# A software pipeline on one core: ScalarE's second exponent ahead of the normalizations, the feed-forward one step later, and GpSimd splitting the negated maxima

## The reference, cut to what matters

```python
x = x + tanh(g_xattn[0]) * L0_xattn(layernorm(x), ctx, ctx)     # 16 heads of 16, softmax, no projections
x = x + tanh(g_ffn[0])   * L0_ffn(layernorm(x), ...)            # scale, round to fp8, 256x256 matmul, rescale, bias
x = x + tanh(g_xattn[1]) * L1_xattn(layernorm(x), ctx, ctx, mask, Wq, bq, Wk, bk, Wv, bv, Wo, bo)
x = x + tanh(g_ffn[1])   * L1_ffn(layernorm(x), weight, gamma, beta)   # fake quantization, ternary weight
```

## Time and profile before

| | |
|---|---|
| median of 3 runs (lowest to highest) | 2249.64 us (2249.06 to 2306.87) |
| profiled execution | 2246.3 us, span 2244.5 us |
| busy: PE, PEld | 1947.8 us (87%), 1429.4 us (64%) |
| busy: DVE, ACT, POOL | 1941.7 us (87%), 1637.9 us (73%), 1122.4 us (50%) |
| first pass, steady part | about 60 to 860 us |
| second pass, steady part | about 890 to 2110 us |

### The profile page before, as it was taken

The page is one execution under the profiler, slowest core; times in us unless marked ns, Lnnn a source line. Parts: engine busy times, 40 slices in busy tenths (PEclk is TensorE's granted clock), DMA queues, the critical chain, the costliest instruction groups (busy, mean ns, idle before and its releaser), DMA issues. The chain is left out here.

```text
span 2244.5 us, 73785 instructions
## 1 busy us (share of the span) xinstructions
PE 1947.8 (87%) x24736; PEld 1429.4 (64%) x24736; DVE 1941.7 (87%) x3958; ACT 1637.9 (73%) x2631; POOL 1122.4 (50%) x1905
## 2 busy tenths in 40 slices
PE   3888888888888886799999999999999999999857
PEld 2665665665665654577777777777777777777545
DVE  4788888888888886589999999999999999999579
ACT  1777777777777776377777777777777777777579
POOL 2566666666666664234444444444444444444310
PEclk8999999999999998799999999999999999999879
DMA  2221211211211110100000000000000000000035
GB/s 79 65 63 59 62 60 59 63 60 59 63 60 59 61 53 13 30 23 24 21 21 21 21 21 21 21 21 21 21 21 21 22 23 21 21 21 18 1 111 189
DMA packets 113869, 95.23 MB, mean 42 GB/s; under 512 B 13440, under 2 KB 113792, under 8 KB 113792
## 3 DMA queue, kind: packets, MB, share of 16 engines
q1 hardware_dynamic: 113792, 94.23, 13.4%
HBM read 60.63 MB, written 33.55 MB: 42 GB/s over the span
## 5 line engine op out<-in xcount | busy, mean ns | idle before, releaser
L844 DVE TENSOR_REDUCE a_nmax<-bank_max 128x8 f32<-128x1024 f32 x512 | 624.8, 1220 | 132.9 <-DVEq L843 127.1
L1113 PE MATMUL bank_max<-UM,U 32*128 32x256 f32 x4096 | 585.7, 403 | 13.7 <-PEq L1226 7.1
L1120 PE MATMUL bank_exp<-UM,U 32*128 32x256 f32 x4096 | 556.7, 389 | 3.9 <-PEq L1261 3.9
L1135 PE MATMUL bank_o<-probs,V 128*17 128x128 f32 x8192 | 325.9, 276 | 170.4 <-PEq L1131 166.3
L641 ACT ACTIVATE probs<-bank_exp 128x1024 f32<-128x1024 f32 x256 | 262.2, 1024 | 272.3 <-ACTq L640 272.3
L1113 PEld LDWEIGHTS bank_max<-UM,U 32*128 32x128 f32 x4096 | 353.1, 185 | 105.6 <-issue 99.6
L1135 PEld LDWEIGHTS bank_o<-probs,V 128*17 128x17 f32 x8192 | 192.0, 96 | 326.2 <-issue 325.4
L530 POOL TENSOR_SCALAR UM<-U,heads_eo 128x512 f32<-128x512 f32 x128 | 88.6, 692 | 605.7 <-POOLq L528 605.7
L1120 PEld LDWEIGHTS bank_exp<-UM,U 32*128 32x128 f32 x4096 | 372.6, 185 | 5.8 <-issue 5.2
L941 DVE CAST bank_max<-ff_qT 128x1024 f32<-128x1024 bf16 x256 | 314.4, 1228 | 8.9
L573 ACT ACTIVATE probs<-bank_exp 128x1024 f32<-128x1024 f32 x256 | 261.8, 1023 | 81.2 <-ACTq L572 81.2
(11 more groups left out here) (168 smaller groups left out, 4252.0 us busy)
## 6 DMA issues: line engine op xcount, KB each, us to landing
X<-in_x SPq DMA_DIRECT2D x128, 128.0 KB, 2.1
ctx<-in_ctx SPq DMA_DIRECT2D x128, 128.0 KB, 2.0
out_y<-U SPq DMA_DIRECT2D x128, 128.0 KB, 1.7
ctx<-out_y SPq DMA_DIRECT2D x128, 128.0 KB, 2.0
out_y<-X SPq DMA_DIRECT2D x64, 256.0 KB, 2.1
ff_qq<-in_mask_BxSxS_ik SPq DMA_DIRECT2D x128, 64.0 KB, 1.8
X<-in_L_xattn_Wq SPq DMA_DIRECT2D x1, 256.0 KB, 2.8
X<-in_L_xattn_Wk SPq DMA_DIRECT2D x1, 256.0 KB, 3.1
```

What stands on the lines that cost most here:

```text
L844: return v.tensor_reduce(a_nmax[:, k2, n * H // 2:(n + 1) * H // 2], max_pair[:, :, :, :].rearrange("p i h t -> p (i h) t"), axis=AX.X, op ...
L1113: last = mm(max_pair[:, r % 2, 2 * c:2 * c + 2, :], U[now][32 * r:32 * r + 32, c, :], UM[now][32 * r:32 * r + 32, DC + c, :, :], start=not ...
L1120: last = mm(exp_pair[:, r % 2, 2 * c:2 * c + 2, :], U[before][32 * r:32 * r + 32, DC + c, :], UM[before][32 * r:32 * r + 32, c, :, :], sta ...
L1135: last = mm(bank_o[32 * j:32 * j + VW, (2 * c + n) * P:(2 * c + n + 1) * P], V[k4][:, 8 * c + 2 * r + e, :], a_probs[n][:, r % 2 * HG + 2 ...
```

## The change

In the first pass ScalarE does its second exponent directly behind `sh_T` (and `ff_y`). The two normalizations that stood ahead of it are spread: one stands behind the second exponent, the other at the start of the following step. The stages of the feed-forward behind its normalization move by one step, so that the rounding grid (L925 to L930) and GpSimd's L493 now fall into even steps, and L885, L897 and L905 into odd steps. In both passes the split of the negated maxima leaves VectorE; GpSimd does the same two operations (`split_shift`), behind V in the first pass and at the end of the step in the second. New semaphores: `max_made` (VectorE to GpSimd) and `ff_read` (VectorE to ScalarE).

```diff
--- before.py
+++ after.py
@@ gpsimd
+            def split_shift(k2):
+
+                pool.wait_ge(max_made, 1)
+                pool.sem_inc(max_made, -1)
+                top = a_nmax[:, k2, :].rearrange("p (i b) -> p i b", i=4)
+                mine(nc.gpsimd.tensor_copy(sh_v[:, :, :, 0], top))
+                settle()
+                nc.gpsimd.tensor_tensor(sh_v[:, :, :, 1], top, sh_v[:, :, :, 0], ALU.subtract).then_inc(shift_made, 1)
...
-                if odd and live(-5):
+                if live(0):
+                    split_shift(k % 2)
+                if not odd and live(-6):
 
                     pool.wait_ge(grid_made, 1)
                     pool.sem_inc(grid_made, -1)
@@ scalar
+                if odd and live(2):
+                    normed(a_xn[1], i + 2, (k // 2 + 1) % 2, 3).then_inc(xn_made, 1)
+                if not odd and live(-5):
+                    normed(ff_xy[:, 1, :], i - 5, (k + 7) // 2 % 2, 1).then_inc(fx_made, 1)
                 if live(-2):
                     exp_pair_of(1)
...
-                if odd and live(-7):
-                    if live(-11):
+                if not odd and live(-8):
+                    if live(-12):
...
+                if live(-2):
+                    exp_pair_of(0)
                 if odd and (live(3) or live(-5)):
                     act.wait_ge(norm_made, 1)
                     act.sem_inc(norm_made, -1)
                 if odd and live(-5):
+                    if live(-7):
+                        act.wait_ge(ff_read, 1)
+                        act.sem_inc(ff_read, -1)
                     normed(ff_xy[:, 0, :], i - 5, k // 2 % 2, 0)
-                    normed(ff_xy[:, 1, :], i - 4, k // 2 % 2, 1).then_inc(fx_made, 1)
                 if not odd and live(2):
-                    for n in range(2):
-                        normed(a_xn[n], i + 2 + n, (k // 2 + 1) % 2, 2 + n).then_inc(xn_made, 1)
-                if live(-2):
-                    exp_pair_of(0)
-                if not odd and live(-6):
+                    normed(a_xn[0], i + 2, (k // 2 + 1) % 2, 2).then_inc(xn_made, 1)
+                if odd and live(-7):
                     act.wait_ge(fq_T, 1)
@@ vector
-                if not odd and live(-6):
+                if odd and live(-7):
 
                     vec.wait_ge(grid_added, 1)
...
                     vec.sem_inc(max_read, 1)
-                    n_hi = mine(v.tensor_copy(sh_v[:, :, :, 0], a_nmax[:, k % 2, :].rearrange("p (i b) -> p i b", i=4)))
+                    vec.sem_inc(max_made, 1)
                 y = a_y[k // 2 % 2]
-                if not odd and live(-8):
+                if odd and live(-9):
...
-                if not odd and live(-8):
+                if odd and live(-9):
                     settle(n_y)
-                    v.scalar_tensor_tensor(xs2(i - 8), y.rearrange("p b n -> p (b n)"), gate[:, 2:3],
-                                           xs2(i - 8), ALU.mult, ALU.add).then_inc(y_used, 1)
-                if live(0):
-                    settle(n_hi)
-                    v.tensor_tensor(sh_v[:, :, :, 1], a_nmax[:, k % 2, :].rearrange("p (i b) -> p i b", i=4),
-                                    sh_v[:, :, :, 0], ALU.subtract).then_inc(shift_made, 1)
+                    v.scalar_tensor_tensor(xs2(i - 9), y.rearrange("p b n -> p (b n)"), gate[:, 2:3],
+                                           xs2(i - 9), ALU.mult, ALU.add).then_inc(y_used, 1)
...
-                if odd and live(-5):
+                if not odd and live(-6):
 
                     vec.wait_ge(fx_made, 1)
...
                     settle()
+                    if live(-4):
+                        vec.sem_inc(ff_read, 1)
                     mine(v.tensor_scalar(a_e.bitcast(U32), a_t.bitcast(U32), EXPONENT, None, ALU.bitwise_and))
@@ vector, step_b
                     settle(n_max)
+                    vec.sem_inc(max_made, 1)
                 if live(1):
                     seed_max((k + 1) % RING)
-                if live(0):
-                    mine(v.tensor_copy(sh_v[:, :, :, 0], a_nmax[:, k % 2, :].rearrange("p (i b) -> p i b", i=4)))
-                    settle()
-                    v.tensor_tensor(sh_v[:, :, :, 1], a_nmax[:, k % 2, :].rearrange("p (i b) -> p i b", i=4),
-                                    sh_v[:, :, :, 0], ALU.subtract).then_inc(shift_made, 1)
```

More of the change, by code:

```diff
@@ L198, in build @@
         max_read = sem("max_read")
+        max_made = sem("max_made")
         shift_made = sem("shift_made")
@@ L215, in build @@
         fx_made = sem("fx_made")
+        ff_read = sem("ff_read")
         m_made = sem("m_made")
@@ L445, in _ @@
             settle()
+            sh_v = sh.rearrange("p (b i r) -> p i b r", b=4, i=4)
+            def split_shift(k2):
[5 more added lines that the diff above has]
+                nc.gpsimd.tensor_tensor(sh_v[:, :, :, 1], top, sh_v[:, :, :, 0], ALU.subtract).then_inc(shift_made, 1)
             def step_a(i, k, live):
@@ L602, in step_a @@
                     act.sem_inc(fy_made, -1)
-                    nc.scalar.activation(a_y[(k - 7) // 2 % 2].rearrange("p b n -> p (b n)"), bank_m[:, :], ACT.Copy,
+                    nc.scalar.activation(a_y[k // 2 % 2].rearrange("p b n -> p (b n)"), bank_m[:, :], ACT.Copy,
                                          scale=scales[:, 3:4]).then_inc(y_out, 1)
+                if live(-2):
+                    exp_pair_of(0)
                 if odd and (live(3) or live(-5)):
@@ L837, in attn_normed @@
                                        ALU.mult)
-            sh_v = sh.rearrange("p (b i r) -> p i b r", b=4, i=4)
             def max_pair_of(n, k2):
@@ L877, in step_a @@
                     vec.sem_inc(attn_x, 1)
-                if not odd and live(-6):
+                if odd and live(-7):
                     vec.wait_ge(grid_added, 1)
                     vec.sem_inc(grid_added, -1)
-                    if live(-8):
+                    if live(-9):
                         vec.wait_ge(fq_used, 1)
```

## The result

The changed kernel takes 2332.84 us (4 runs, 2329.07 to 2336.8) against 2252.97 us before: a ratio of 1.0367, with a 95% interval of 1.0337 to 1.0397. It is 3.7% slower, where no change was forecast (2250 us, 2225 to 2287). The profiled execution has a span of 2331.0 us against 2244.5, 86.5 us more. From the first L844 of a pass to its last, the first pass takes 886.7 us (before 826.8) and the second 1207.5 us (before 1182.5): 60 us come from the first pass, 25 from the second. Some executions of the unchanged kernel also take 2305 to 2317 us; what adds that time is told under "Second pass", and the ratio above leaves out the one of them that is among the four behind 2252.97.

The account below looks back on a forecast made before the run. Chains of waits bound the first pass, PE the second (95% busy). 2246.3 - 1 (loop) + 0 (split, ACT, second pass) + 1 (end) = 2246.3 us profiled, 2250 us on the median's scale, range 2225 to 2287.

Parts of the forecast that it names:

- the views and the loop: First pass: the new pair is set by a chain through GpSimd of 12.89 us, against 12.91 before; given 80%.
- Step 2: GpSimd's leg, first pass: grid, L493, statistics, copies, L478 end at 11.48 us; DVE waits about 1.1 us ahead of L902.
- The masked copies: First pass: UM's m_made holds back the even fill by only 0.3 us, covered by the 12.89 us loop.
- GpSimd's split under cover: Added split on GpSimd, twice per pair: 0.6 us taken, bounds 0.4 to 1.6, expected to cost nothing.
- step 1: PE, ACT and DVE alone, first pass: pair of 11.89 us, 1.02 less; L902 placed 1.37 us behind L844.
- no idle time ahead of L902 in even steps: Sign of a right forecast, DVE in the first pass: about 1 us idle there in odd steps, none in even ones.
- rival B: Slower, first pass: L885 and L897 stretch GpSimd's statistics or copies; two meetings give 13.79 us, 2304 us; 8%.
- The rule weighed in the prediction: GpSimd's SBUF interfaces are shared with VectorE; two-input or two-port VectorE instructions contend, so L470 may lengthen in odd steps.
- The signal to L922: Signal from the end of L478 to DVE's L902, first pass: 0.2 us taken, bounds 0.18 and 0.39.
- B's meetings: L885 or L897 running beside GpSimd's statistics, L470, L472 or L478: one costs 0.45 us, two 0.9 us per pair.
- The second pass: Split moved from DVE to GpSimd there: 0 us change, bounds -4 and +8 us.
- The view of the present path in the prediction's first part: First pass before: late exponents (0.75 and 0.39 us) and two small DVE operations lie on the path; DVE last at even L844.

Follow-up runs that it names:

- e5: Changed kernel with two spare GpSimd additions of 4 elements ahead of the power in the odd step's statistics: 14.95 us per pair in the mean, first pass 943.3 us.
- e6: Changed kernel with two spare GpSimd additions in the even step, ahead of the wait for the grid: 14.03 us per pair in the mean, first pass 889.6 us.
- e8: Changed kernel with GpSimd's statistics moved to the even step, between split and L508: 12.61 us per pair, ratio to the kernel before 1.0108.
- e1: Changed kernel with the split given back to VectorE in both passes: 13.82 us in most first-pass pairs, 14.12 in the mean.
- e2: Kernel before with only the split of the maxima moved to GpSimd, in both passes: 12.92 us per pair.
- e9: Kernel before with the second exponent ahead of the normalizations and, in the first pass, the split on GpSimd: 12.41 us per pair.
- e10: Changed kernel with ff_qq moved behind the odd step's second maxima: 14.71 us per pair.
- e7: Kernel before with only the second exponent moved ahead of the normalizations: 12.40 us per pair, 2215.97 us, ratio 0.9855.

## Why the prediction was wrong

*Right:* the views and the loop. Step 2 named the path that sets the new period (grid, L508, statistics, copies, L491, `x_added`), and e5, e6 and e8 show it. The masked copies do hold back the even fill, by 1.09 us (0.3 forecast), under the cover of the loop, as step 2 said. Right too: the exponents 1.4 us behind their fill, about 1 us of idle time ahead of L922 in odd steps (1.50), the statistics directly behind L508, GpSimd's split under cover (0.6 us, e1 and e2), and a second pass whose steps stay at 18.53 us per pair.

*Wrong:* the steps that failed are terms of the sum of that loop, 12.89 us placed and 13.72 measured, and the turn of the loop, which had no term. By terms:

- L864 to L922: 1.67, placed 1.37 in step 1, +0.30. I put L902 where L891 had stood, although L902 itself stood 1.65 us behind the maxima (402.77 to 404.42 in the earlier trace rows); e9 shows that the cast was not what kept it back. The sign "no idle time ahead of L902 in even steps" was wrong with it: there are 0.45 us.
- L467 to L483: 2.34, placed 1.96 in step 2, +0.38. This is rival B's stretch: the power beside `ff_qq`, which I had waved off because the power touches only 4 elements. e10 shows that it is contention: the power alone costs 0.49, less 0.11 in the small operations around it. The rule weighed in the prediction is borne out by this trace: the Trainium skill, GPSIMD Engine Reference, section 1 (Specifications), names VectorE instructions with two SBUF inputs, and `ff_qq` is one.
- L483 to the end of L491: 2.21, placed 2.05, +0.16, in L485 (0.85 beside L917).
- L929 to the end of the grid: 1.65, placed 1.54, +0.11; the new `ff_read` increment stands between L941 and L946.
- The signal to L922 0.25, placed 0.20; L925 to L864 0.74, placed 0.87; the rest -0.04 together. Sum: +0.83.

I took none of B's meetings into the forecast, only one into the upper end of the range, and gave two of them 8%; two came, worth 0.38 and 0.16 us on the path, and the queue's 0.30 came on top.

- Not placed at all: the turn of the loop, in every fourth pair. The changed kernel's pair there is 14.63 us, 0.9 more. DVE at the turn:

```profile
403.17 0.17 DVE L929 BATCH_NORM_AGGREGATE a_stat<-st6f 128x2 f32<-128x6 f32 x1
404.06 1.23 DVE L864 TENSOR_REDUCE a_nmax<-bank_max 128x8 f32<-128x1024 f32 x1 [0.71 <-DVEq L863]
```

L864 follows L929 after 0.89 us instead of 0.09. Before, the turn cost 0.18 us (DVE before):

```profile
431.81 0.43 DVE L930 TENSOR_SCALAR spare<-spare 128x512 f32<-128x512 f32 x1
432.65 1.23 DVE L844 TENSOR_REDUCE a_nmax<-bank_max 128x8 f32<-128x1024 f32 x1 [0.41 <-DVEq L843]
```

There L844 follows the start of the last operation after 0.84 us, nearly as in the changed kernel, but 0.67 of it are there in every pair: the longer L930 and 0.24 us of idle time. In e7, without that idle time, the turn costs 0.34 us. So the change put a short operation, on the path, ahead of the turn; why the turn takes as long as it does is open. Over the pairs: 62 x (14.01 - 12.98) = 64 us by the means, 60 us in the pass.

- The second pass: 0 was right for the change, but 25 us of the measured difference are stalls that the profiled execution before had not (the other times of the changed kernel lie within 4 us of its profiled one). A changed kernel without them would be at about 2308 us, 2.7% above the profiled execution before, and still outside the range. Why the executions of some kernels nearly always have them and those of e7 had none in five times is open; so is what each starts from.

The view of the present path in the prediction's first part was half right: the late exponent was on it (e7 gains 31 us in the pass), the two small VectorE operations were not (e2). The sentence that failed there was that DVE is the last at the even L844; it was PE, by some 0.12 us.

## What to carry to other kernels

When work moves to an engine with idle time, lay its new order out as a loop and sum that loop, through every engine that waits for it; an engine that is busy for 50% of the whole time (66% of this pass) can come to set the period. An operation that sits behind a wait is often free, because the queue's waits and increments take as long: look at what starts next in a row without it before taking its duration off. Before building a change of three parts, try the one-line part alone: here it gave 1.5%, and with the parts built around it the change lost 3.7%.

## What the runs showed of the hardware

The stalls of the second pass go with the instruction queue. In all 14 profiled executions the packets of q8 above 45 are 9 times the number of long stretches (63, 90, 99, 108, 117, 126, 144 and 153 packets; 2, 5, 6, 7, 8, 9, 11 and 12 stretches, without an exception), and a stretch costs 2.6 to 7.6 us. It fits that PE's loop body is fetched anew in that turn: per turn PE and its weight loads run some 1600 instructions (13223 and 13224 in 1200 us), every other engine at most 110. Which engine q8 serves is argued from these numbers and from the place of the packets around PE's wait, and was not tried.

Contention between VectorE and GpSimd is not bound to large tiles: a power over 128 x 4 elements went from 1.02 to 1.51 us beside one VectorE operation of 0.65 us. And a repeated PE wait of 1.64 us, where the changed kernel has 1.09, came with 22 stretches at the lower clock in the pass instead of 3, though most of the single waits were not followed by one.
